# Two expert blocks rewritten as one straight-line program each: no loops, no inner barriers, one pass of statistics

## What is computed

```
x = x + slot_attention(layernorm(x))      # stage A
x = x + expert_block(layernorm(x))        # stage B
x = x + full_attention(layernorm(x))      # stage C
x = x + expert_block(layernorm(x))        # stage D, the same weights as B

def expert_block(x):                      # x is already normalised once by the caller
    a = attention(layernorm(x) * w1 + b1) # 16 heads of 128, rope on q and k, causal softmax, out @ wo + bo
    h = x + a
    y = layernorm(h) * w2 + b2
    raw = softmax(y @ w_gate)             # 4 experts
    comb = softmax over the two largest of raw, 0 elsewhere
    m = sum over e of comb[e] * (gelu(y @ we1[e] + be1[e]) @ we2[e] + be2[e])
    return h + m
```

## Time and profile before

| | |
|---|---|
| median of 3 runs | 2762.05 us (2761.68 to 2763.11) |
| profiled execution | 2761.43 us |
| its span on the core | 2759.6 us |
| busy share | PE 86%, DVE 62%, ACT 44%, POOL 39% |
| stages by their first instruction | A from 0, B from 1376.1, C from 1949.0, D from 2182.4 us |
| mean granted TensorE clock | 0.947 of 2.4 GHz |

### The profile page before, as it was taken

How to read it: one execution, slowest core, us unless ns; L and a number is a source line. 1 busy time by engine, 2 the same in 40 slices (tenths; PEclk the granted TensorE clock), 3 DMA queues, 4 the chain that set the end, 5 groups by cost and what they waited for, 6 DMA issues and landing times. The chain is left out here.

```text
span 2759.6 us, 50938 instructions
## 1 busy us (share of the span) xinstructions
PE 2370.4 (86%) x18448; PEld 1638.4 (59%) x18448; DVE 1700.9 (62%) x3330; ACT 1203.0 (44%) x2945; POOL 1082.0 (39%) x1240
## 2 busy tenths in 40 slices
PE   6888898888878888888559999998889589999988
PEld 3477655776567844687336656675433255666675
DVE  4767686687857778577346766713557356766622
ACT  3645465555545554554224444502225244444411
POOL 0377534773447732676224434400310034444300
PEclk9999999999999999999779999998989889999989
DMA  2100001000000000000040000000100310000000
GB/s 52 42 2 2 2 16 35 2 2 10 16 28 2 3 9 8 17 2 2 2 107 18 17 17 11 6 1 0 47 1 1 79 36 18 17 17 6 6 0 16
DMA packets 74983, 46.64 MB, mean 17 GB/s; under 512 B 27416, under 2 KB 68256, under 8 KB 74400
## 3 DMA queue, kind: packets, MB, share of 16 engines
q1 hardware_dynamic: 74784, 43.95, 5.7%
HBM read 42.89 MB, written 1.05 MB: 16 GB/s over the span
## 5 line engine op out<-in xcount | busy, mean ns | idle before, releaser
L1148 DVE SCALAR_TENSOR_TENSOR work<-four,taps,work 128x511 f32<-128x511 f32 (+2 forms) x384 | 284.6, 747 | 124.0 <-ACT work L844 114.5
L1567 POOL TENSOR_TENSOR rot<-q_plain,ropes 128x512 f32<-128x512 f32 x66 | 83.6, 1267 | 697.3 <-ACT q_plain L1589 697.3
L594 PE MATMUL four<-xT,wring 128*128 128x512 f32 x512 | 252.7, 620 | 6.8 <-DMA wring<-in_Wk_dram 4.7
L901 ACT ACTIVATE work<-four 128x512 f32<-128x512 f32 x216 | 129.0, 597 | 270.9 <-PE four L673 244.8
L1538 DVE TENSOR_REDUCE nmaxf<-four 128x1 f32<-128x512 f32 (+3 forms) x256 | 125.7, 491 | 165.4 <-PE four L1464 158.5
L724 PE MATMUL four<-work 128*128 128x128 f32 x1536 | 217.3, 286 | 0.0
L1607 ACT ACTIVATE pr<-four,nmaxf 128x512 f32<-128x512 f32 (+3 forms) x256 | 133.9, 525 | 178.8 <-DVE nmaxf L1538 175.6
L1462 PE MATMUL four<-rot,rot 128*128 128x512 f32 (+3 forms) x512 | 191.0, 469 | 11.8 <-ACT oT L1402 6.1
L724 PEld LDWEIGHTS four<-work 128*128 128x128 f32 x1536 | 193.6, 196 | 3.9
L1083 POOL TENSOR_TENSOR work<-work 128x256 f32<-128x256 f32 x184 | 146.1, 794 | 77.7 <-DVE work L1212 58.0
L1090 POOL TENSOR_TENSOR work<-work 128x256 f32<-128x256 f32 x184 | 141.6, 769 | 84.0 <-PE bank L758 74.3
(11 more groups left out here) (244 smaller groups left out, 5425.5 us busy)
## 6 DMA issues: line engine op xcount, KB each, us to landing
wqkv<-in_f_wq_dram SPq DMA_DIRECT2D x34, 128.0 KB, 2.2
wqkv<-in_f_wk_dram SPq DMA_DIRECT2D x34, 128.0 KB, 2.2
wqkv<-in_f_wv_dram SPq DMA_DIRECT2D x34, 128.0 KB, 2.2
wo<-in_f_wo_dram SPq DMA_DIRECT2D x2, 2048.0 KB, 11.3
we<-in_f_we_dram SPq DMA_DIRECT2D x4, 1024.0 KB
wring<-in_Wk_dram SPq DMA_DIRECT2D x4, 512.0 KB, 3.8
wring<-in_Ww_dram SPq DMA_DIRECT2D x4, 512.0 KB, 5.8
wring<-in_Wv_dram SPq DMA_DIRECT2D x4, 512.0 KB, 3.7
```

The source lines that it names most:

```text
L594: last = nc.tensor.matmul(unit_bank(i)[:], wring[n % 2][:, c, h * P:(h + 1) * P], k.xT[:, c, b * T:(b + 1) * T], start=(c == 0), stop=(c = ...
L1148: ins = nc.vector.scalar_tensor_tensor(out=cbuf[i % 4][:, n:], in0=unit_bank(i)[:, 0:T - n], scalar=taps[:, {"q": 0, "k": 1}.get(kind, 2), ...
```

## The change

`expert_block` becomes one block, with one program per engine from the first statistics to the last add, and without hardware loops. In its order:

- Norm vectors, q/k/v biases and be1 are laid out on the host, so that each is one plain DMA (`f_ln`, `f_bqkv`, `f_be1`). SyncE's order is now: norm vectors, head 0, biases, causal mask, ropes, heads 1 to 3, bo, wo, gate and expert weights, then each further head. Each consumer waits for a semaphore of its own (`ln_in`, `f_const`, `bo_in`, `wo_in`, `m_in`).
- The statistics of x are taken once. `hid` is (x - m) / sqrt(v + eps); `nrm`, the norm of `hid`, is computed from the same m and v with (x - m) / sqrt(v (1 + eps) + eps^2).
- Transposes, copies and projections of the first unit go by half (one half is one batch).
- The 32 units are unrolled, the order inside a unit is the same, and the 33rd is gone.
- bo is added to `hid` by POOL behind the q rotation of units 2 to 9; `hid` is added to x by POOL per tile.
- Output row 0 stands ahead of the outputs of the last unit; output rows use two banks; the second norm's transposes of half 0 stand behind output row 4.
- Gate, hidden units of experts 0 and 1 and the second norm go by half; hidden units have four banks in place of two.
- In stage D each half of x is stored when its last adds are done, within the block.

The core of the diff:

```diff
+    a["f_ln"] = np.ascontiguousarray(np.stack(norms).transpose(2, 0, 1))
+    a["f_bqkv"] = np.ascontiguousarray(np.stack(biases).transpose(2, 0, 1))
+HIDDEN = [(e, ic, half) for half in range(2) for e in range(2) for ic in range(IC)] + \
+         [(e, ic, half) for e in range(2, E) for ic in range(IC) for half in range(2)]
-        layer_norm(k, k.x, hid, False, loads=constants_and_weights)
-        layer_norm(k, hid, nrm, True, ln[:, 0], ln[:, 1], (f_const, 160))
+        out_bank = lambda t: k.bank[(7, 5)[t % 2]]
+        hidden_bank = lambda n: k.bank[(4, 2, 3, 5)[n % 4]]
         with nc.Block() as block:
+            # sync
+                sp.dma_start(ln[:], d["f_ln"]).then_inc(ln_in, 16)
+                load(0)
+                sp.dma_start(bqkv[:], d["f_bqkv"]).then_inc(f_const, 16)
+                sp.dma_start(causal[:], d["c_causal"]).then_inc(f_const, 16)
+                sp.dma_start(ropes[:], d["c_rope"]).then_inc(f_const, 16)
+                for head in range(1, HEADS):
+                    load(head)
...
+                for head in range(HEADS, FH):
+                    sp.wait_ge(v_made, (head - HEADS + 1) * B)
+                    load(head)
+                if rows is not None:
+                    for half in range(2):
+                        sp.wait_ge(y_used, E * NT + 4 * half + 4)
+                        sp.dma_start(rows[:, 4 * half:4 * half + 4], k.x[:, 4 * half:4 * half + 4]).then_inc(stored, 16)
+                    sp.wait_ge(stored, 32)
+            # tensor
+                turn_x(0)
+                project(0, 0)
+                turn_x(1)
+                project(0, 1)
+                values(0)
+                pe.wait_ge(masks_in, 2)
+                for u in range(UNITS_B):
+                    more = u + 1 < UNITS_B
+                    scores(u, 0)
+                    scores(u, 1)
+                    if more:
+                        project(u + 1, 0)
+                    scores(u, 2)
+                    if more:
+                        project(u + 1, 1)
+                    scores(u, 3)
+                    turn(u, 0)
+                    turn(u, 1)
+                    if u:
+                        outputs(u - 1)
+                    if more:
+                        values(u + 1)
+                    turn(u, 2)
+                    turn(u, 3)
+                output_rows(0)
+                outputs(UNITS_B - 1)
+                for t in range(1, NT):
+                    output_rows(t)
+                    if t == 4:
+                        turn_hid(0)
+                gate(0)
+                for n in range(4):
+                    hidden(n)
+                turn_hid(1)
+                gate(1)
+                for n in range(4, 8):
+                    hidden(n)
+                pe.wait_ge(combed, 1)
...
+            # vector
+                for t in range(NT):
+                    last = nc.vector.bn_stats(k.stats[:, t, :], k.x[:, t, :])
...
+                nc.vector.tensor_scalar(roots[:, 0], k.mean_var[:, :, 1], 1.0 + EPS, EPS * EPS, ALU.mult, ALU.add)
+                nc.vector.tensor_scalar(roots[:, 1], k.mean_var[:, :, 1], EPS, None, ALU.add).then_inc(x_var, 1)
...
+                for t in range(NT):
+                    dve.wait_ge(out_made, t + 1)
+                    dve.wait_ge(hid_biased, t + 1)
+                    nc.vector.tensor_tensor(hid[:, t], hid[:, t], out_bank(t)[:, 0:D], ALU.add).then_inc(h_added, 1)
+                    nc.vector.bn_stats(k.stats[:, t, :], hid[:, t, :]).then_inc(h_stats, 1)
+                    nc.vector.bn_aggr(k.mean_var[:, t, :], k.stats[:, t, :]).then_inc(h_stats, 1)
+                    if t % 4 == 3:
...
+            # gpsimd
+                for u in range(UNITS_B):
+                    rope_q(u)
+                    if 2 <= u < 2 + NT:
+                        t = u - 2
+                        pool.wait_ge(bo_in, 16)
+                        pool.wait_ge(hid_made, t + 1)
+                        nc.gpsimd.tensor_tensor(hid[:, t], hid[:, t], bo[:], ALU.add).then_inc(hid_biased, 1)
+                for t in range(NT):
+                    pool.wait_ge(h_added, t + 1)
+                    nc.gpsimd.tensor_tensor(k.x[:, t], k.x[:, t], hid[:, t], ALU.add).then_inc(x_joined, 1)
```

More of the change, by code:

```diff
@@ L1331, in sem @@
             return k.sem(name + r)
-        HEADS = 4
-        BODY = HEADS * B
         hid = sb("hid", [P, NT, D])
@@ new lines, in values @@
+                def values(u):
+                    h, b = unit_head(u)
+                    if u:
+                        pe.wait_ge(v_kept, u)
+                    for t in range(CH):
+                        for c in range(DC):
+                            last = nc.tensor.matmul(k.bank[1][:, t * P:(t + 1) * P], k.xT[:, c, b * T + t * P:b * T + (t + 1) * P],
+                                                    wqkv[h % HEADS][:, 2, c, :], start=(c == 0), stop=(c == DC - 1))
+                    last.then_inc(v_made, 1)
@@ new lines, in outputs @@
+                def outputs(u):
+                    pe.wait_ge(p_kept, (u + 1) * CH)
+                    pe.wait_ge(v_kept, u + 1)
+                    if u >= 1:
+                        pe.wait_ge(o_kept, u)
+                    for t in range(CH):
+                        last = nc.tensor.matmul(k.bank[6][:, t * P:], vv[u % 2][:, t, :], pT[u % 2][:, t, t * P:],
+                                                start=(t == 0), stop=(t == CH - 1))
+                    last.then_inc(o_made, 1)
@@ L1675, in _, with gate @@
+                def gate(half):
                     pe.wait_ge(m_in, 80)
-                    for t in range(NT):
+                    pe.wait_ge(xT_kept, DC * half + DC)
+                    for t in range(4 * half, 4 * half + 4):
                         for c in range(DC):
@@ new lines, in hidden @@
+                def hidden(n):
+                    e, ic, half = HIDDEN[n]
+                    if n >= 4:
+                        pe.wait_ge(h_kept, n - 3)
+                    elif n == 1:
+                        pe.wait_ge(s_exp, UNITS_B * CH)
+                    elif n == 3:
+                        pe.wait_ge(h_added, NT)
+                    for c in range(DC):
+                        last = nc.tensor.matmul(hidden_bank(n)[:], we1[:, e, c, ic * P:(ic + 1) * P],
+                                                k.xT[:, c, half * 512:half * 512 + 512], start=(c == 0), stop=(c == DC - 1))
+                    last.then_inc(h_made, 1)
@@ L2073, in build @@
         stored = k.sem("stored")
+        rows = out.rearrange("b (c p) n -> p (b c) n", p=P)
         with nc.Block() as block:
```

734 lines of the change are left out of this document (364 added, 370 removed).

## The result

The changed kernel takes 2631.3 us (median of 4 runs, 2627.8 to 2633.2), the kernel before 2762.6 beside it: a ratio of 0.952, 95% interval 0.9508 to 0.9532. The profiled execution took 2630.3 us with a span of 2628.5. The forecast was 2640 us, with a range of 2629 to 2654.

A forecast was written before the change was run, and what follows sets the result against it. TensorE alone was taken to set the unit's 11.25 us, with barriers and loop boundaries adding waits. Savings less 5.8 for POOL's adds sum to 121.6: 2761.4 - 121.6 = 2639.8, plus 0.6 for the median, 2640 us; range 2629 to 2654.

The forecast's parts named there:

- Start: Start of each expert block: first score 19.8 us after the first statistics (S), saving 25.2 and 26.0 us.
- Rival (b): Block start bound by transfers: constants or weights come 3 to 6 us late per block, 2646 to 2652; chance 0.15.
- Loops: Thirty units per block: the three loop boundaries cost 15.8 and 16.3 us, and 32.1 us go.
- Rival (d): Loop boundaries: the loss is the maximum, exp and scaling chain's and returns elsewhere, plus 32, 2672; chance 0.05.
- Waits on constants instead of registers: Steady units: replacing register waits gains nothing, since TensorE has no idle time in six units.
- POOL's adds: Adds of bo in units 2 to 9: 0.36 us each, sixteen times, 5.8 lost; bounds 0 to 0.8 each.
- rival (a): POOL's adds of bo each win over waiting VectorE, 0.8 x 16, 2647, or find a gap, 2634; chance 0.15.
- Last unit and rows: After the last unit's first score: output row 0 at +8.3, end at +66.9; saves 4.3 per block, 8.6.
- Gate and experts: Stretch up to the first bias row: 21.4 us against 38.5, saving 17.1 per block, 34.2.
- rival (c): Clock falls in the thinned stretches: some 2 to 4 us at one to three places, 2644 to 2650; chance 0.12.
- Store: Final store: half the rows leave earlier, the last transfer is smaller, a barrier goes; 1.3 us saved, once.
- Rival (e): Unrolled units: an engine supplied with instructions too slowly stretches every unit, 2640 + 160 = 2800; chance 0.03.

The follow-up runs named there:

- run 2: Changed kernel, no loop, but the old loop's order and copy wait at units 8, 16 and 24: units take 363.5 and 361.9 us, 16.1 and 14.2 more.
- run 1: Changed kernel with TensorE alone looping units 8 to 23, waits in registers: units 350.1 and 350.2 us instead of 347.4 and 347.7.
- run 6: Changed kernel with the heads' weights loaded last, no barrier: first score 33.9 and 32.8 us after the first statistics, 14.6 and 13.6 more.
- run 7: Changed kernel with the second norm in one piece behind output row 7: output row 0 to first bias row 86.2 and 89.1 us, 6.0 and 7.2 more.
- run 5: Changed kernel with two passes of statistics again, no barrier: first score 25.96 us after the first statistics in both blocks, 6.7 more.
- run 8: Changed kernel with VectorE's scaling of row 3 moved ahead of its k add: 2618.3 us, ratio 0.9475.
- run 3: Changed kernel with POOL's adds of bo waiting until VectorE has scaled the previous unit's last row: units 2 to 9 take 11.08 us.
- run 11: The changed kernel itself, unchanged, measured again: 2628.4 us, ratio 0.9503 to the kernel before.
- run 4: Changed kernel with POOL's eight adds of bo left out: units of a block 346.9 and 346.8 us, 0.5 and 0.9 less.
- run 9: Changed kernel with three waits filled (POOL's bo adds later, transposes of half 1 and of comb each one hidden unit earlier): 2620.0 us, ratio 0.9482.
- run 10: Changed kernel with the three filled waits of run 9 and the scaling ahead of the k add: 2608.8 us, ratio 0.9437.

## Why the prediction was right, step by step

The direction and the size came from reading each stage by its own stretches, and most terms held. The profiled execution was 9.5 us faster than the sum (2639.8 against 2630.3). That is 13.2 too little saved in the units, 3.4 in start, rows and store, less 2.8 too much in gate and experts, less 4.3 of scatter and small terms. The result lies near the lower edge of the range, and part of that is luck: stage A happened to take 4.0 us longer. Without this the profiled execution would have taken 2626.3 us, below the range.

How much of the cause is shown: stages B and D together became 135.1 us shorter (131.1 and the 4.0 of stages A and C). Put back by runs are 30.3 (run 2, the order at the loop boundaries), about 6 (run 1, its 0.10 us taken for 60 units), 28.2 (run 6, the loads) and 13.2 (run 7, the norm by half), some 78 in all. The barriers at the start (24), the rest of gate and experts (18), the last unit and the output rows (10), the rest of the units (3) and the store (2) were put down to the change by reading the stretches, and no run tries them alone.

**Start**: forecast the first score at S + 19.8, measured S + 19.3; the named releasers were right, and ropes was there in time. Rival (b), transfers, fell. The start of the projection was forecast at S + 8.6 and measured there, though the parts named for it add up to 8.4. Run 6 gives what the loads' order costs by itself, 14 us, and run 5 what the second pass costs, 6.7; the two do not add, and what the barriers cost is open.

**Loops**: "the three boundaries cost 15.8 and 16.3" held: run 2 puts 16.1 and 14.2 back without a loop. The forecast took the size from the length of thirty units and the cause from TensorE's waits; it is now shown that the order of the outputs product causes them, and that the branch costs 0.2 to 0.5 us. Of run 2's 16.1 us 3.4 are the clock, which fell behind two of the three boundaries, as it did in the kernel before. Rival (d), that the loss would come back elsewhere, fell: what it rested on, the 2.09 us for the scaling, belongs to the boundary itself.

**The step that failed: "Waits on constants instead of registers I cost at nothing: in the six units TensorE has no idle time that they could give back."** Steady units went from 11.25 to 11.14 us, 60 x 0.11 = 6.6 us over both blocks, and run 1 puts 0.10 of the 0.11 back with TensorE's waits alone. The fault lies in the reading. Busy time of 67.49 in 67.49 us does not say that TensorE works at its own limit, as a busy TensorE holds small stretched matmuls too (1.10 us for a pair that takes 1.03); run 8 goes on to 11.03 with the same reading. The sign of it stood in the earlier trace rows: a weight load that waited 0.18 us for the scaling.

**The second mis-sized term: POOL's adds at 5.8 us; measured 1.4.** I had put POOL's add behind the k add and the scaling behind both. In fact the add starts before the k add ends, takes 0.3 us more than alone, and is over 0.08 us before the scaling ends. The unit pays 0.15 for the meeting and gets 0.06 back (run 3): 0.09 a unit, within the bounds of 0 to 0.8, and next to the low case of rival (a), 2634. This and the register waits make 4.4 + 6.6 = 11.0 of the 13.2 us; the other 2.2 lie in the first units, whose steps differ by the clock: in stage B the first score ran at 2.04 us a pair before and at 1.10 after.

The Trainium skill, "SBUF — State Buffer", section "Who interferes with whom", says that the loser at the shared ports is blocked for the whole instruction. The trace agrees roughly. The scaling takes 0.28 us alone and ends 0.08 behind POOL's add in run 8; the k add takes 0.68 to 0.73 alone and ends 0.55 behind it in the changed kernel. So each must have begun its work 0.13 to 0.20 us before POOL's printed end (spans on POOL are rough).

**Last unit and rows**: forecast row 0 at +8.3 and the end at +66.9, measured +7.7 and +66.0.

**Gate and experts**: forecast 21.4 twice, measured 21.8 and 23.5. The forecast counted one idle copy; the second wait, 1.15 us for ScalarE's copy of comb, was in the 2.2 us taken over from before. ScalarE's table load between the second exp and the gelu took 1.28 us, and the gelu began 1.29 after its start (1827.72, 1829.01), not on the path, as forecast. The 1.7 us of stage D are rival (c), the clock. In run 11, the same kernel, stage B took 80.2 us from output row 0 to the first bias row and stage D 83.5. Its chance of 0.12 was low: both profiles of the changed kernel show it in one block of two, at 1.7 and 3.4 us, and over the nine profiles in which this stretch has the changed kernel's code it is nine blocks of 18.

**Store**: 1.3 against 1.8. **Rival (e)**, instruction supply: the straight-line units are the shorter ones; it fell.

## What to carry to other kernels

A busy share of 100% on TensorE is no proof that it sets the time: compare the step of a repeated unit with the sum of its matmuls at their shortest duration, and look for a weight load that waits a tenth or two for another engine, because that engine's chain may then be the bound; moving the instruction, as in run 8, decides it. Before a loop is unrolled for its boundary, look whether it is the order at the boundary that costs; it could perhaps also be mended inside the loop, which no run tried. And put an instruction that other engines wait for at once ahead of one that a port holds up anyway.

## What the runs showed of the hardware that was not expected

- A small wait can cost more than itself. The stretch from the last output row to the first bias row, with its waits of 1.19 and 1.15 us, has the same code in nine profiles (the changed kernel twice, runs 1 to 6 and 8). In 18 blocks it took 21.8 us at a granted clock of 1.00 nine times, 23.5 at 0.93 four times and 25.2 at 0.86 five times. Behind the wait of 2.12 us (run 2) the clock fell three times of six, behind 3.30 (run 7) both times. With the waits filled (runs 9 and 10) it stayed at 1.00 in all four blocks. If half of the blocks fell whatever the waits, four of four at 1.00 would still come once in sixteen, so that the waits cause the fall is likely and not shown.
- Waits on register values, some twenty in a unit with about six register instructions for them, cost TensorE 0.1 us in 11.1, though none shows as idle time.
- POOL began its first product 0.76 us after the start of the copy of q in units where it had just done another add, and 0.83 us in those where it had not. In the kernel before it was 0.76 without any add.
- VectorE's instruction of 0.28 us lasted 1.02 when it met POOL's add, yet the whole unit became shorter by 0.11: what counts is which of the two instructions is held.
